# Statistics of x taken earlier in VectorE's chunk, normalisation gated earlier on GpSimd, and the guard's range turned ahead of the last value products

## What is computed

```python
def attn(x, Wq, Wk, Wv, memory, memory_norm, memory_weight):   # x is the layer-normed input
    q, k, v = x @ Wq.T, x @ Wk.T, x @ Wv.T                      # 512, 128, 128 wide
    probs = softmax(einsum('bsqhd,bthd->bqhst', qh, kh) * scale)  # 4 queries x 8 heads of 16
    a_dot = einsum('bqhst,bthd->bsqhd', probs, vh)
    sigma_q = elu(q)
    a_mem = sigma_q @ memory / (sigma_q @ memory_norm)
    w = sigmoid(memory_weight)
    return a_dot * (1 - w) + a_mem * w
x = x + attn(layernorm(x), ...)
x = x + ffn(layernorm(x), fp8 weight, scales)
```

## Time and profile before

| | |
|---|---|
| median of 3 executions | 2065.53 us (2063.67 to 2066.37) |
| the profiled execution | 2066.21 us, its span 2064.5 us |
| busy over the span | TensorE 98%, ScalarE 94%, VectorE 54%, GpSimd 7% |
| 50 to 75 us, of 25.00 us | TensorE 22.06, VectorE 15.07, GpSimd 12.58, ScalarE 11.79 |
| the same stretch, granted clock | 0.86 |

### The profile page before, as it was taken

One profiled execution on the slowest core, in us unless ns is written; L12 is line 12 of the kernel. 1 busy time (PEld: TensorE's weight loads), 2 busy tenths in 40 slices (PEclk: granted clock), 3 DMA queues, 4 the chain that ended last, 5 costly groups with the idle time before them and its releaser, 6 DMA issues.

```text
span 2064.5 us, 63537 instructions
## 1 busy us (share of the span) xinstructions
PE 2016.5 (98%) x27828; PEld 972.8 (47%) x27828; DVE 1117.6 (54%) x1731; ACT 1938.5 (94%) x2191; POOL 136.0 (7%) x166
## 2 busy tenths in 40 slices
PE   7887999999999999999999999999999999999998
PEld 6666434434444444444444444444444444444445
DVE  6565655544555545555455554555544555545555
ACT  5545899999999999999999999999999999999997
POOL 5545000000000000000000000000000000000000
PEclk9888999999999999999999999999999999999999
DMA  5545411111111211122111221112111222121111
GB/s 188 171 153 178 134 40 48 48 48 38 43 51 51 71 39 37 49 50 71 49 34 49 71 51 51 30 45 69 51 51 38 64 51 51 51 58 38 49 50 46
DMA packets 137687, 131.68 MB, mean 64 GB/s; under 512 B 31619, under 2 KB 113947, under 8 KB 137435
## 3 DMA queue, kind: packets, MB, share of 16 engines
q1 hardware_dynamic: 136571, 126.25, 22.0%
q10 hardware_dynamic: 864, 1.57, 0.2%
HBM read 86.57 MB, written 37.49 MB: 60 GB/s over the span
## 4 chain that ended last, share of the span: by engine, by line
PE 92%; DVE 3%; POOL 2%; issue 1%; ACT 1%; POOLq 0%; DVEq 0%; ACTq 0%; PEldq 0%
PE ps L920 42%; PE ps L981 42%; PE ps L812 3%; POOL xn L585 2%; PE ps L1021 1%; PE ps L1005 1%; PE ps L785 1%; DVE stats L1148 1%; PE ps L1074 1%; PE ps L1091 1%; DVE x_low L1177 0%; DVE parts L1210 0%; POOL rstd L578 0%; DVE ps L1302 0%; ACT parts L680 0%
## 5 line engine op out<-in xcount | busy, mean ns | idle before, releaser
L747 ACT ACTIVATE pool<-ps 128x1024 f32<-128x1024 f32 x1953 | 1794.9, 1153 | 5.6 <-PEq L957 2.0
L920 PE MATMUL ps<-q_st,k_st 99*32 99x512 bf16 x16128 | 1109.7, 379 | 1.9 <-DVE wide L1367 1.6
L981 PE MATMUL ps<-pool,v_st 128*32 128x512 f32 (+1 forms) x8568 | 1069.0, 567 | 0.0
L920 PEld LDWEIGHTS ps<-q_st,k_st 99*32 99x32 bf16 x16128 | 470.8, 96 | 782.5 <-issue 470.9
L981 PEld LDWEIGHTS ps<-pool,v_st 128*32 128x32 f32 x8568 | 288.5, 110 | 191.0 <-issue 0.2
L1416 DVE STREAM_TRANSPOSE by_token<-ps 128x512 f32<-128x512 f32 x63 | 45.2, 717 | 476.6 <-PE ps L981 476.6
L1409 DVE SCALAR_TENSOR_TENSOR late<-late 128x1024 f32<-128x1024 f32 x189 | 231.6, 1225 | 6.5
L1395 DVE TENSOR_SCALAR late<-ps 128x512 f32<-128x512 f32 x126 | 87.2, 692 | 127.6 <-PE ps L920 127.6
L627 POOL TENSOR_TENSOR var_eps<-moments,eps 128x1 f32<-128x1 f32 x32 | 6.1, 190 | 1810.6 <-DVE moments L1445 1810.6
L1472 DVE SCALAR_TENSOR_TENSOR y_out<-ps,scalars,resid 128x512 f32 (+1 forms) x28 | 21.0, 751 | 112.6 <-PE ps L1005 112.6
L1411 DVE SCALAR_TENSOR_TENSOR pool<-late 128x1024 f32<-128x1024 f32 x63 | 77.2, 1226 | 2.2
(11 more groups left out here) (150 smaller groups left out, 1069.0 us busy)
## 6 DMA issues: line engine op xcount, KB each, us to landing
q_st<-q_aug SPq DMA_DIRECT2D x384, 64.0 KB
v_st<-v_aug SPq DMA_DIRECT2D x64, 256.0 KB
q_aug<-parts SPq DMA_DIRECT2D x96, 128.0 KB
k_st<-k_aug SPq DMA_DIRECT2D x64, 192.0 KB
sigma_kept<-y_out SPq DMA_DIRECT2D x32, 256.0 KB, 4.3
k_st<-k_aug SPq DMA_DIRECT2D x64, 128.0 KB
wqT<-sigma_kept SPq DMA_DIRECT2D x32, 256.0 KB, 3.3
resid<-in_x SPq DMA_DIRECT2D x7, 1024.0 KB, 7.6
```

The source lines that it names most:

```text
L747: act.activation(held[:, half_u * 2 * CH:half_u * 2 * CH + 2 * CH], sc[unit % SLOTS].rearrange("p a b -> p (a b)"), ACT.Exp, scale=EXP_UNIT)\
L920: last = pe.matmul(dst[VW * c:VW * c + VW, :], k_st[0:AUG, par, keys:keys + VW], q_st[0:AUG, par, q * CH:q * CH + CH], start=True, stop=True)
L981: last = pe.matmul(acc[par][VW * c:VW * c + VW, :].rearrange("v (i s) -> v i s", s=VW)[:, places, :], v_st[:, par, j, :], by_place[:, c, p ...
```

## The change

- VectorE: statistics and mean of chunk c+2 stand in chunk c ahead of strip o = 3's work, where before the statistics stood at the end of chunk c and the mean at the start of chunk c+1. Those of chunk 1 stand before chunk 0.
- GpSimd: reciprocal deviation and normalisation of chunk c+2 stand at the end of chunk c, and no longer at the start of chunk c+1. In its list of instructions the order is the same as before; only the waits' sources move. Of chunk 1 it normalises two tiles, VectorE the other two.
- SyncE: x is loaded a chunk earlier, after the parts of strip 2 instead of the chunk's start.
- TensorE, last chunk: the key norms stand after 3 instead of 6 value products, and the range is turned ahead of the last 3 value products instead of behind them. VectorE sums the keys ahead of the last maximum.

```diff
 def store_parts(c, par):                       # SyncE
-    if c + 2 < NG:
-        sp.wait_ge(x_loaded[par], 16 * (c // 2) + 16)
-        load_x(c + 2, par)
+    if c == 0:
+        load_x(2, 0)
...
+        if o == 2 and c + 3 < NG:
+            sp.wait_ge(x_loaded[1 - par], 16 * ((c + 1) // 2) + 16)
+            load_x(c + 3, 1 - par)
...
 def chunk(c, par, last, first_guard=False):    # GpSimd
     for o in range(QG + 1):
-        if o == 0 and not last:
-            rstd_of(c + 1, 1 - par)
-            normalise(c + 1, 1 - par)
...
+    if c + 2 < NG:
+        rstd_of(c + 2, par)
+        normalise(c + 2, par)
 rstd_of(0, 0)
 pool_e.wait_ge(rstd_ready, 1)
+rstd_of(1, 1)
+normalise(1, 1, TPC // 2)
...
 def turn_xn(c, ks):                            # TensorE
     pe.wait_ge(xn_ready, c + 1)
+    if c == 1:
+        pe.wait_ge(xn_rest_ready, 1)
...
-    project(c - 1, 1 - par, V_STRIP, range(KT // 2))
+    project(c - 1, 1 - par, V_STRIP, range(1))
     key_norms(c)
-    project(c - 1, 1 - par, V_STRIP, range(KT // 2, KT))
+    project(c - 1, 1 - par, V_STRIP, range(1, KT))
...
-    project(c, par, V_STRIP, range(2, KT))
+    project(c, par, V_STRIP, range(2, KT - 1))
     pe.wait_ge(range_ready, 2)
     for b in range(BATCH):
         last = pe.transpose(ranges_turned[:, b, :], bound[:, 6, b:b + 1], ident[:, :])
     last.then_inc(ranges_ready, 1)
+    project(c, par, V_STRIP, range(KT - 1, KT))
...
 def chunk(c, par, first_guard=False):          # VectorE
-    dve.wait_ge(stats_ready, c + 2)
-    mean_and_variance(1 - par)
...
+        if o == QG - 1 and c + 2 < NG:
+            dve.wait_ge(x_loaded[par], (c - par) * 8 + 32)
+            statistics(c + 2)
+            dve.wait_ge(stats_ready, c + 3)
+            mean_and_variance(par)
...
+            normalise(1, range(TPC // 2, TPC), xn_rest_ready)   # chunk 0, after strip 0
...
     largest_norm(c, 0)
-    if c + 2 < NG:
-        dve.wait_ge(x_loaded[par], (c - par) * 8 + 32)
-        statistics(c + 2)
...
-    largest_norm(c, 1)                         # last chunk
     sum_keys(c)
+    largest_norm(c, 1)
```

More of the change, by code:

```diff
@@ L269, in attention_ffn @@
         xn_ready = sem("xn_ready")
+        xn_rest_ready = sem("xn_rest_ready")
         tp_ready = sem("tp_ready")
@@ L578, in rstd_of, with normalise @@
                 pool_e.tensor_tensor(rstd[:, par, :], var_eps[:, :], minus_half[:, :], ALU.pow).then_inc(rstd_ready, 1)
-            def normalise(c, par):
+            def normalise(c, par, tiles=TPC):
                 pool_e.wait_ge(rstd_ready, c + 1)
                 pool_e.wait_ge(tp_ready, c * KT)
-                for t in range(TPC):
+                for t in range(tiles):
                     last = pool_e.tensor_scalar(xn[:, t, :], resid[:, c * TPC + t, :], moments[:, par, t, 0:1],
@@ L1154, in mean_and_variance, with normalise @@
                 last.then_inc(moments_ready, 1)
[L1156 to L1159, removed]
+            def normalise(c, tiles, done):
+                dve.wait_ge(rstd_ready, c + 1)
+                dve.wait_ge(tp_ready, c * KT)
+                for t in tiles:
+                    last = dve.tensor_scalar(xn[:, t, :], resid[:, c * TPC + t, :], moments[:, c, t, 0:1], rstd[:, c, t:t + 1],
                                              ALU.subtract, ALU.mult)
-                last.then_inc(xn_ready, 1)
+                last.then_inc(done, 1)
             def split_weight(j):
@@ L1183, in _ @@
             split_weight(0)
-            normalise_first()
+            normalise(0, range(TPC), xn_ready)
             split_weight(1)
@@ L1193, in _ @@
             statistics(1)
+            dve.wait_ge(stats_ready, 2)
+            mean_and_variance(1)
             def weights_of_memory():
@@ L1353, in last_chunk @@
                 largest_norm(c, 0)
+                sum_keys(c)
                 largest_norm(c, 1)
-                sum_keys(c)
                 guard_sums(1)
```

## The result

The changed kernel takes 2031.55 us (median, 2029.85 to 2032.55), the kernel before 2065.95 beside it: a ratio of 0.983, 95% interval 0.982 to 0.985, 34.4 us less. The prediction had 2024, range 2018 to 2032. The direction and the place of the gain were right; some 7 us of the 41.8 did not come, and the time lies only 0.45 us inside the range, at the price that the rivals B and C had. Only the trace tells which account holds.

The account below looks back on a forecast made before the run. The prediction took TensorE's waits for the normalised chunk, with slow products after them, as the bound (ceiling 50 us). A gain of 41.8 us from 2066.21 gave 2024.4, about 2024 us, range 2018 to 2032.

Parts of the forecast that it names:

- the 41.8: Up to the last chunk's first product: total gain of 41.8 us, with the last chunk and attention adding nothing.
- B: VectorE in chunks 0 and 4: GpSimd's normalisation blocks it, costing 1.3 and about 5 us; 2031 us, chance 0.13.
- C: GpSimd stays last, TensorE still waits for xn, 1 to 1.5 us a chunk for six; 2031 us, chance 0.08.
- The ring: Chunk loop of keys, VectorE's end of chunk, statistics, GpSimd, turn, keys: period 27.14 us between key-norm products.
- the new period: Steady chunk: 20.4 us between key norms, TensorE reaching them at about 19.5 and waiting some 0.9 on VectorE's maximum.
- key norms at 37.42: Chunk 0: VectorE without a gap for 13.16 us from strip 1's sigma, maximum at 36.59, key norms at 37.42.
- The 1.6 us of slow products: Chunk 4: after TensorE's 3.7 us wait behind the guard, products at the lower clock add 1.6 us, bounds 0 and 2.5.
- Nothing to 2 us, I take nothing: SyncE, chunk 5's guard stores: a late store could hold ScalarE's first parts of the last chunk; charged at zero.
- three products now lie under them: Last chunk: the 1.63 us ahead of the first scores are VectorE's flag, now covering three products; last chunk taken at nothing.
- The hold of 0.7 us on the key norms: Last chunk: key norms stand three products earlier but need the query norms' unmoved maximum, so TensorE holds 0.7 us.
- A: Steady chunks: VectorE's row is shorter than counted and TensorE bounds the period at 19.5 us; 2018 us, chance 0.12.
- D: Every chunk: TensorE's 0.9 us halts keep it at the lower clock, 16 us a chunk; some 2104 us, chance 0.02.

Follow-up runs that it names:

- two kernels with parts put back: Changed kernel with VectorE's means returned to the next chunk's start: 2046.62 us; with the statistics also returned behind the chunk's maximum: 2062.78 us.
- kernel with all four edits: Changed kernel with chunk 0's statistics later, first two splits earlier in later chunks, prefetch later, first guard's work behind chunk 4's maximum: 2022.05 us.
- fastest kernel: Changed kernel with the four small edits, plus statistics in VectorE's gaps at strips 0 and 1 of chunks 1 to 5: 2021.08 us.

## Why the prediction was right, and where it was not

**Right: the mechanism of the gain.** The ring was keys, VectorE's end of chunk, statistics, GpSimd, turn. The two kernels with parts put back show it: the period is 27.2, 23.6 or 20.6 us as the means end behind the mark, ahead of it, or ahead of the squares of the keys. GpSimd was in time, with no wait for xn.

**Right in part by luck: the new period.** The prediction added 19.5 us of TensorE and 0.9 of waiting for VectorE's maximum; the changed kernel has 19.7 and 0.91 of waiting for a split. Two numbers agree, and the wait is another one. Even with that wait cut, the wait on the maximum is 0.2 us and not 0.9, because TensorE needs 0.2 to 0.3 more than the prediction gave it and still waits 0.3 for the split.

**The first scores came at 187.50, predicted near 180.5.** The 7.0 us are these, place by place:

- *Chunk 0: 3.7 us (41.14 for 37.42).* The prediction has VectorE without a gap to the maximum and the "key norms at 37.42", and let only the maximum be waited for. But TensorE's second half-turn needs the first half's split, since TensorE turns a tile only when the split of the tile before it is done (`turn_xn` waits for `x_low_ready`), and the statistics stood ahead of that split in VectorE's row: 3.06 us, and slow products after it. I had added the statistics to VectorE's row, and not asked who waits for the instructions that they push back (ten in a steady chunk; the "eleven" ahead of the prediction is one too many). With the statistics of chunk 0 behind the first splits, 2.4 us of it were gone, 3.0 counted from the start of the first turn.
- *The period: 20.6 for 20.39, 0.65 us in three chunks.* The same omission. The half-turn waits 0.91 for a split behind strip 2's last part. With this wait cut to 0.30, VectorE's row is the bound as predicted, at 20.3.
- *Chunk 4: 23.69 for 23.21, 0.5 us more, and then 1.4 less.* The guard costs what it should within 0.5. TensorE waits 2.74 us there, for 3.7 predicted. The 1.6 us of slow products, taken with bounds of 0 and 2.5, did not come in the changed kernel's trace; they did in others.
- *Chunk 6: 15.03 for 13.8 from the mark to the last chunk's first product (162.25), 1.2 us.* The half-turn's wait again, 0.91.
- *The last chunk: 25.25 for 22.88, 2.4 us.* Of these, 1.5 us are late stores: "Nothing to 2 us, I take nothing" was the wrong end. Before, SyncE's queue had issued the prefetches and stood still from 195.8 to 199.3; with chunk 6 some 6 us shorter (15.03 for 20.99) it has no such pause, and the stores behind the nine prefetches are late. With the prefetches moved, the turn of the range comes 15.29 us behind chunk 6's mark, as before the change. The other 0.8 us are the step "three products now lie under them": the flag comes no earlier, 16.2 us behind chunk 6's mark as before, since the hold on the key norms uses up what the turn's place gains; but the take of the last values, which those three products push back, ends at 17.0 us for 16.1 (with the later prefetch, 184.73 - 167.72; before, 221.06 - 204.97), and so is the last. From the turn of the range to the first scores it is 2.83 us for 2.01, in every kernel with the edits at the end of the stage 2.8 or more, and 2.00 where they are put back. The hold of 0.7 us on the key norms is there as predicted.

3.7 + 0.65 + 0.5 - 1.4 + 1.2 + 2.4 = 7.05.

The kernel with all four edits is a test of this list as a whole, but for the 0.8 us at its end. It has chunk 0's mark at 37.68 and chunk 3's at 98.60, where the prediction has 37.42 and 98.59. That the second agrees to 0.01 is luck: three periods are 60.92 us for 61.17, and the first turn of an execution starts anywhere from 10.8 to 12.4 us. But VectorE's row was counted rightly, and what was missing stood beside it.

**The rivals.** *A* gave the period as TensorE's 19.5; in the fastest kernel TensorE alone needs 19.7, and in the changed one the wait for the split came on top. *B*, GpSimd's normalisation blocks VectorE, is nearly nothing. In chunk 0 VectorE's two tiles of xn ran while GpSimd wrote its own two, and only a two-input instruction, which before took 0.14 under the same normalisation, stretched clearly:

```profile
21.41 1.00 DVE L1168 TENSOR_SCALAR xn<-resid,moments,rstd 128x512 f32<-128x512 f32 x2
...
23.23 0.47 DVE L1216 TENSOR_TENSOR scalars<-scalars 128x1 f32<-128x1 f32 x1
```

```profile
20.68 4.33 POOL L588 TENSOR_SCALAR xn<-resid,moments,rstd 128x512 f32<-128x512 f32 x2
```

That is 1.00 for 0.92 on VectorE, 4.33 for 4.12 on GpSimd, and 0.3 at 23.23; the guard's rows in chunk 4 took 1.32 for the 0.87 of the later guard's. Together that is about 1 us, where B had 7. The Trainium skill, SBUF — State Buffer, section "Who interferes with whom", calls the shared pair of ports an exclusive lock, for which a VectorE instruction with two SBUF inputs contends with a GpSimd instruction that reads SBUF, and of a VectorE instruction in a two-port mode and GpSimd it says that the later one blocks fully. For GpSimd's squares the traces agree: a two-input instruction started at 118.78 while they ran (118.49 to 119.53), took 0.76 in place of 0.15, and ended with them. For the normalisation they do not: the one at 23.23 ended at 23.70, in the middle of GpSimd's second tile (some 22.8 to 25.0). VectorE's two tiles were not held until GpSimd's tile was through either; they read one tensor, and whether they ran in a two-port mode no run shows. *C* fell with the waits for xn. *D* too: the clock reads 1.00 from 50 to 187 us although TensorE halts 0.9 us in each chunk.

## What to carry to other kernels

When work is moved into a row of an in-order engine, look not only at the row's end but at each instruction that it pushes back and at who waits for it; the row's length was right here to 0.04 us, and the wait in its middle was missed. When one engine's waits vanish, a queue that used them as pauses can become late: look at what is issued between two stores that something waits for. Where two things are waited for, look at both: the edit at the end of the stage left the flag where it was and made the take of the values the later one. And test small gains together, when each is about as large as the spread.

## What the runs showed of the hardware

A wait of the same length did not always leave the lower clock behind it. TensorE waited 2.74 to 2.75 us for the maximum of chunk 4 in six kernels with nearly the same instructions around it. In the changed kernel and in that with the later prefetch the clock then stayed at 1.00; in four others it fell, as in the second line here (118 to 138 us; PE, clock, DMA), the first being the changed kernel:

```profile
118.00:138.00 20.00, 16.36 (x82) 1.00 0.55 176
```

```profile
118.00:138.00 20.00, 16.39 (x74) 0.91 0.51 162
```

That costs 1.2 to 1.6 us a time (21.79 to 22.15 for 20.57 between two marks), as much as three of the four small edits brought by themselves, or more. Ahead of chunk 0's second half-turn, a wait of 2.65 to 3.67 us was followed by slow products in six kernels, and in one it was not. Nor was a longer wait the surer one: with the means put back, four waits of 2.4 to 3.0 us for xn each left slow products (clock 0.86 over 12 us from each of these turns on). Waits of 0.9 us and less left the clock alone in every kernel. What decides in between, no run here shows.
